# Expert phase of an attention and mixture-of-experts block: second layer with stationary weights, weights and biases fetched by transfers inside the chip

## The reference

```python
x = x + layernorm(attention(layernorm(x), w_kv_down, w_kv_up, w_q, w_out))
x = x + layernorm(ffn(layernorm(x), centroids, gamma, beta, W1, b1, W2, b2))

def ffn(x, ...):            # 8 experts, F = 512
    expert = argmax(feats @ centroids.T)            # one expert for each token
    alpha  = sigmoid(sum(feats * centroids[expert]))
    # the sublayer of expert e:
    #   h = layernorm(xs) * gamma[e] + beta[e]
    #   xs + relu(h @ W1[e].T + b1[e]) @ W2[e].T + b2[e]
    return alpha * y_expert + (1 - alpha) * feats
```

## Time and profile before

| what | value |
|---|---|
| median of 3 runs | 1291.23 us (1290.55 to 1293.27) |
| profiled execution, its own time | 1290.58 us |
| its span, first to last instruction | 1286.4 us |
| PE busy | 1221.9 us, 95% |
| DVE, ACT, POOL busy | 1130.4, 1062.5, 924.2 us |
| expert phase | from the first load of rows at 1101.8 us to the end of the span |

### The profile page before, as it was taken

The page is one execution under the profiler, slowest core; times in us unless marked ns, Lnnn a source line. Parts: engine busy times, 40 slices in busy tenths (PEclk is TensorE's granted clock), DMA queues, the critical chain, the costliest instruction groups (busy, mean ns, idle before and its releaser), DMA issues.

```text
span 1286.4 us, 42145 instructions
## 1 busy us (share of the span) xinstructions
PE 1221.9 (95%) x12784; PEld 1105.4 (86%) x12785; DVE 1130.4 (88%) x4457; ACT 1062.5 (83%) x3244; POOL 924.2 (72%) x1495
## 2 busy tenths in 40 slices
PE   7999999999999999999999999999999997599992
PEld 6888888888888888888888888888888886599982
DVE  5999999999999999999999999999999995488873
ACT  4999898999999999999999999999999893466661
POOL 4577777777777777777777777777777665067775
PEclk8999999999999999999999999999999997799997
DMA  5000000000000000000000000000000003333320
GB/s 228 6 10 18 16 16 16 16 16 16 16 16 16 16 16 16 16 16 16 16 16 16 16 16 16 13 16 14 15 16 13 15 15 123 98 97 101 96 84 13
DMA packets 39233, 43.03 MB, mean 33 GB/s; under 512 B 4802, under 2 KB 35398, under 8 KB 38800
## 3 DMA queue, kind: packets, MB, share of 16 engines
q1 hardware_dynamic: 33536, 29.43, 7.6%
q0 software_dynamic: 5648, 13.00, 2.7%
HBM read 25.16 MB, written 18.16 MB: 34 GB/s over the span
## 4 chain that ended last, share of the span: by engine, by line
PE 86%; issue 5%; POOL 3%; DVE 1%; ACT 1%; SPq 1%; DMA 1%; POOLq 0%; ACTq 0%; DVEq 0%
PE psZU L682 17%; PE psS L605 14%; PE psZU L697 14%; PE psP L649 10%; PE psZU L685 7%; PE psT L619 5%; PE psT L620 5%; PE psT L621 5%; PE psS L292 3%; POOL out L456 2%; PE psZU L306 2%; PE psT L306 1%; PE psP L584 1%; PE psM L736 1%; PE psM L727 1%
## 5 line engine op out<-in xcount | busy, mean ns | idle before, releaser
L1219 POOL TENSOR_TENSOR softmax<-softmax,rinv 128x256 f32<-128x256 f32 (+1 forms) x512 | 413.2, 828 | 213.8 <-DVE rinv L947 213.0
L781 ACT ACTIVATE softmax<-softmax,nmax 128x128 f32<-128x128 f32 (+1 forms) x1024 | 453.8, 451 | 9.1 <-DVE nmax L923 8.3
L923 DVE CUSTOM_DVE_ANT_0 softmax<-psS,mask 128x128 f32<-128x128 f32 (+1 forms) x1024 | 321.6, 352 | 5.6 <-PE psS L605 1.1
L932 DVE TENSOR_TENSOR p_both<-psP,p_both 128x768 fp32r<-128x768 f32 x256 | 243.8, 952 | 0.9 <-ACT p_both L745 0.9
L745 ACT ACTIVATE t_hi<-psT 128x512 fp32r<-128x512 f32 x256 | 153.0, 598 | 84.0 <-PE psT L621 78.0
L911 DVE TENSOR_TENSOR t_lo<-psT,t_hi 128x512 fp32r<-128x512 f32 x256 | 175.3, 685 | 41.9 <-ACT t_hi L745 40.8
L745 ACT ACTIVATE p_both<-psP 128x768 fp32r<-128x768 f32 x256 | 206.6, 807 | 2.3 <-PE psP L649 2.3
L781 ACT ACTIVATION_READ_ACCUMULATOR softmax<-softmax,nmax 128x1 f32 x1024 | 199.1, 194 | 0.0
L952 DVE TENSOR_TENSOR z_lo<-psZU,z_hi 128x512 fp32r<-128x512 f32 x256 | 175.3, 685 | 20.0 <-ACT z_hi L745 18.1
L605 PE MATMUL psS<-t_hi,t_lo 64*128 64x128 f32 (+1 forms) x1024 | 164.5, 317 | 0.4 <-DVE nmax L923 0.4
L682 PE MATMUL psZU<-p_both,xk_hi 128*128 128x512 f32 x512 | 160.7, 395 | 0.0
(11 more groups left out here) (197 smaller groups left out, 3192.0 us busy)
## 6 DMA issues: line engine op xcount, KB each, us to landing
softmax<-routed_rows SPq DMA_DIRECT2D x39, 260.0 KB, 2.7
routed_rows<-padr SPq DMA_DIRECT2D x8, 520.0 KB, 4.9
wx<-ffn_w SPq DMA_DIRECT2D x2, 2058.0 KB, 13.0
xin<-x SPq DMA_DIRECT2D x32, 128.0 KB, 2.2
xres<-x SPq DMA_DIRECT2D x32, 128.0 KB, 2.1
out<-wq_s,ids POOLq DMA_INDIRECT x78
wup_s<-wup SPq DMA_DIRECT2D x1, 1024.0 KB, 5.9
routed_rows<-pay,dst POOLq DMA_INDIRECT x64
```

Of the source, the lines that this page charges most:

```text
L781: last = nc.scalar.activation(prob[:, pb, h, a:z], nscore[:, (s - lag) % 2, h, a:z], ACT.Exp, bias=nmax[:, pb, h, q:q + 1], scale=-1.0, ac ...
L923: last = v.tensor_tensor_reduce(nscore[:, n1, h, a:z], psS[:, h, a:z], mask[:, a:z], -1.0, -MASKED, ALU.add, ALU.min, nmax[:, p1, h, q:q + 1])
L932: v.tensor_tensor(by_half(p_lo, s % 2), psPh, by_half(p_hi, s % 2).bitcast(F32), ALU.subtract).then_inc(S["p_split"], 1)
L1219: last = g.tensor_tensor(pr, pr, rinv[:, p2, :, q:q + 1].broadcast_to([P, 2, z - a]), ALU.mult)
```

## The change

PE now takes the second layer's weights as stationary operand and the hidden activations, 256 tokens wide, as the moving one, for tile s-2. The result `psY` has channels on the partitions. ACT adds the bias b2, one number for each partition, while it copies the result to `yt` (tile s-3), and PE turns `yt` back (two transposes to `psO`, tile s-3). DVE's part with gain and statistics is now for tile s-4, DVE's and ACT's normalisation and POOL's add for tile s-5, POOL's scatters for tile s-6. There is one slot more at the end (`rest + 6`).

The weights no longer come by ACT copies or by PE's addressing. SP issues two more transfers for each tile, from SBUF to SBUF: the split W1 of the expert into `w1st` (two buffers, 4096 bytes for each partition), and b1, W2 and b2 together into `w2st` (four buffers, 2068 bytes for each partition). It reads the expert from `table` once for both. The first waits until the first layer of the tile before last is done, the second until the tile four earlier has left its buffer. `b2row`, `picks` and `b1st`, and all that prepared them (L711, L745 with `b2row`, L1012 and L1014), are gone. Left out of the diff below are the renumbered lags of DVE and POOL and DVE's lines of `b2row`.

```diff
@@ -261,13 +261,26 @@
                     sp.wait_ge(S["pad_stored"], 16 * E)
                 sp.dma_start(fin[:, s], rows[bass.ds(row, T), :].rearrange("(t p) c -> p t c", p=P)
                              ).then_inc(f_loaded[s], 16)
+                if live(2):
+                    sp.wait_ge(S["h_done"], m0 + s - 1)
+                elif s == 0:
+                    sp.wait_ge(S["w1_split"], E)
+                e = sp.value_load(table[0:1, bass.ds(m0 + s, 1), 1], min_val=0, max_val=E - 1)
+                sp.dma_start(w1st[:, s % 2].rearrange("p m f -> p (m f)").bitcast(F32),
+                             w1[:, bass.ds(e, 1)].rearrange("p a m f -> p (a m f)").bitcast(F32)
+                             ).then_inc(w1_loaded[s % 2], 16)
+                if live(4):
+                    sp.wait_ge(S["yt_ready"], m0 + s - 3)
+                    sp.wait_ge(S["relu_d"], m0 + s - 3)
+                elif s == 0:
+                    sp.wait_ge(S["bias_added"], 1)
+                sp.dma_start(w2st[:, s % 4, :], wx[:, bass.ds(e, 1), B1:].rearrange("p a c -> p (a c)")
+                             ).then_inc(w2_loaded[s % 4], 16)
 
             ffn_phases(sp, slot)
 
         def ffn_pe(pe):
             mm = nc.tensor.matmul
-            pe.wait_ge(S["table_ready"], 1)
-            pe.wait_ge(S["b2_split"], 1)
 
             def slot(m0, n0, s, live):
                 if live(0):
@@ -277,12 +290,10 @@
                     for t in range(2):
                         last = nc.tensor.transpose(psN[:, t * P:(t + 1) * P], fin[:, s, t, 0:P], ident[:])
                     last.then_inc(S["n_tr"], 1)
-                if live(2):
-                    e = pe.value_load(table[0:1, bass.ds(m0 + s - 2, 1), 1], min_val=0, max_val=E - 1)
                 if live(1):
 
                     pe.wait_ge(S["nt_ready"], m0 + s)
-                    pe.wait_ge(S["w1st_ready"], m0 + s)
+                    pe.wait_ge(w1_loaded[(s - 1) % 2], 8 * m0 + 16 * ((s + 1) // 2))
                     if live(2):
                         pe.wait_ge(S["relu_a"], m0 + s - 1)
                         pe.wait_ge(S["relu_d"], m0 + s - 1)
@@ -292,21 +303,26 @@
                             last = mm(psH[:, j, :], w1st[:, b, m, j * P:(j + 1) * P], nt[:, b, :],
                                       start=(n == 0), stop=(n == 2))
                     last.then_inc(S["h_done"], 1)
-                if live(2):
-
-                    pe.wait_ge(S["relu_a"], m0 + s - 1)
-                    pe.wait_ge(S["relu_d"], m0 + s - 1)
+                if live(3):
+
+                    pe.wait_ge(S["yt_ready"], m0 + s - 2)
                     if live(4):
                         pe.wait_ge(S["g_steps"], 2 * (m0 + s - 3) - 1)
                     for t in range(2):
-                        y = psY[s % 2][:, t, 0:P]
-                        mm(y, picks[:], b2row[:, bass.ds(e, 1), :].rearrange("p a c -> p (a c)"), start=True, stop=False)
-                        for j in range(FB):
-                            a = W2 + j * P
-                            last = mm(y, hid[:, s % 2, j, t * P:(t + 1) * P],
-                                      wx[:, bass.ds(e, 1), a:a + P].rearrange("p a c -> p (a c)"),
-                                      start=False, stop=(j == FB - 1))
-                    last.then_inc(S["y_done"], 1)
+                        last = nc.tensor.transpose(psO[:, t, 0:P], yt[:, t * P:(t + 1) * P], ident[:])
+                    last.then_inc(S["y_tr"], 1)
+                if live(2):
+
+                    pe.wait_ge(S["relu_a"], m0 + s - 1)
+                    pe.wait_ge(S["relu_d"], m0 + s - 1)
+                    pe.wait_ge(w2_loaded[(s - 2) % 4], 4 * m0 + 16 * ((s + 2) // 4))
+                    if live(3):
+                        pe.wait_ge(S["yt_ready"], m0 + s - 2)
+                    for j in range(FB):
+                        a = FB + j * P
+                        last = mm(psY[:, 0, :], w2st[:, (s - 2) % 4, a:a + P], hid[:, s % 2, j, :],
+                                  start=(j == 0), stop=(j == FB - 1))
+                    last.then_inc(S["yt_done"], 1)
 
             ffn_phases(pe, slot)
 
@@ -323,33 +339,28 @@
                     if live(2):
                         act.wait_ge(S["h_done"], m0 + s - 1)
                     cp(nt_hi[:, s % 2, :], psN[:, 0:T]).then_inc(S["nt_hi_done"], 1)
-                if live(4):
-                    b, sf = s % 2, (s - 4) % FU
-                    act.wait_ge(S["gmv_ready"], m0 + s - 3)
+                if live(3):
+                    act.wait_ge(S["yt_done"], m0 + s - 2)
+                    if live(4):
+                        act.wait_ge(S["y_tr"], m0 + s - 3)
+                    nc.scalar.activation(yt[:], psY[:, 0, :], ACT.Identity,
+                                         bias=w2st[:, (s - 3) % 4, W2W - 1:W2W]).then_inc(S["yt_ready"], 1)
+                if live(5):
+                    b, sf = (s - 5) % 2, (s - 5) % FU
+                    act.wait_ge(S["gmv_ready"], m0 + s - 4)
                     for t in range(2):
                         last = nc.scalar.activation(gsd[:, b, t:t + 1], gmv[:, b, t, 1:2], ACT.Sqrt,
                                                     bias=fin[:, sf, t, C_EPS:C_EPS + 1])
                     last.then_inc(S["gsd_ready"], 1)
-                if live(0):
-                    e = act.value_load(table[0:1, bass.ds(m0 + s, 1), 1], min_val=0, max_val=E - 1)
-                    if live(2):
-                        act.wait_ge(S["h_done"], m0 + s - 1)
-                    cp(w1st[:, s % 2].rearrange("p m f -> p (m f)"),
-                       w1[:, bass.ds(e, 1)].rearrange("p a m f -> p (a m f)")).then_inc(S["w1st_ready"], 1)
                 if live(1):
                     act.wait_ge(S["h_done"], m0 + s)
-                    act.wait_ge(S["b1st_ready"], m0 + s)
+                    act.wait_ge(w2_loaded[(s - 1) % 4], 4 * m0 + 16 * ((s + 3) // 4))
                     if live(3):
-                        act.wait_ge(S["y_done"], m0 + s - 2)
+                        act.wait_ge(S["yt_done"], m0 + s - 2)
                     for j in range(2):
                         last = nc.scalar.activation(hid[:, (s - 1) % 2, j, :], psH[:, j, :], ACT.Relu,
-                                                    bias=b1st[:, (s - 1) % 4, j:j + 1])
+                                                    bias=w2st[:, (s - 1) % 4, j:j + 1])
                     last.then_inc(S["relu_a"], 1)
-                if live(0):
-                    if live(4):
-                        act.wait_ge(S["relu_d"], m0 + s - 3)
-                    cp(b1st[:, s % 4, :], wx[:, bass.ds(e, 1), B1:W2].rearrange("p a c -> p (a c)")
-                       ).then_inc(S["b1st_ready"], 1)
 
             ffn_phases(act, slot)
 
...
@@ -705,12 +716,6 @@
                     first_bias(range(s - 1, s))
                 if not live(0) and s == 7:
                     first_bias(range(E // 2, E))
-                if not live(0) and s == 4:
-                    pe.wait_ge(S["nmax_ready"], 2 * PAIRS * NB)
-                    for e in range(E):
-                        last = mm(psS[:, e // 4, (e % 4) * P:(e % 4 + 1) * P],
-                                  wx[:, e, B2:B2 + 1].broadcast_to([P, P]), ident[:], start=True, stop=True)
-                    last.then_inc(S["b2_turned"], 1)
                 if s == 1 and not live(2):
                     pe.wait_ge(S["xn_ready"], 2)
                     turn_x()
@@ -798,11 +803,6 @@
                     if live_b(2):
                         act.wait_ge(S["a_tr"], b0 + db - 1)
                     cp(at[:], psU[:, 0:T]).then_inc(S["u_copied"], 1)
-                if not live(0) and s == 5:
-                    act.wait_ge(S["b2_turned"], 1)
-                    for n in range(2):
-                        last = cp(b2row[:, 4 * n:4 * n + 4, :].rearrange("p e c -> p (e c)"), psS[:, n, :])
-                    last.then_inc(S["b2_hi_done"], 1)
                 if live(0):
                     act.wait_ge(S["t_ready"], g0 + s + 1)
                     if live(2):
...
```

More of the change, by code:

```diff
@@ L195, in block_kernel @@
             "p (b m f) -> p b m f", b=2, m=2)
[L196 to L199, removed]
+        W2W = FB + FB * P + 1
+        w2st = sb("w2st", [P, 4, W2W])
         assert 2 * HD == 2 * FB * T and HD // P == 2 * FB
         hid = wup_s[:].rearrange("p (b j t) -> p b j t", b=2, j=FB)
+        yt = sb("yt", [P, T])
         gst = sb("gst", [P, 2, 6])
@@ L206, in block_kernel @@
         grs = sb("grs", [P, 2, 2])
-        for n in """pads_ready pad_stored ends_ready table_steps table_ready w1_hi_done w1_split w1st_ready b1st_ready
-            b2_turned b2_hi_done b2_split
-            nt_hi_done nt_ready relu_a relu_d n_tr h_done y_done g_steps gmv_ready gsd_ready
+        for n in """pads_ready pad_stored ends_ready table_steps table_ready w1_hi_done w1_split
+            nt_hi_done nt_ready relu_a relu_d n_tr h_done yt_done yt_ready y_tr g_steps gmv_ready gsd_ready
```

(49 more changed lines are left out.)

24 lines of the change are left out of this document (11 added, 13 removed).

## The result

Median 1305.67 us after (1302.58 to 1307.37, 4 runs), 1292.22 before on the same chip (1290.55 to 1293.27, 4 runs): ratio 1.0114, 95% interval 1.0098 to 1.0131. By the medians the change costs 13.5 us, where I had forecast 3.3. The profiled execution took 1307.3 with a span of 1302.9, against 1290.58 and 1286.4 before.

The account below looks back on a forecast made before the run. It took a loop over POOL's scatters with late PE signals, 3.89 us a tile, as the bound, not PE's 3.6. -3.2+0.9+1.7+1.7+2.2=+3.3 on 1291.2 gave 1294.5 us, range 1281 to 1315.

Parts of the forecast that it names:

- Ahead of the phase: Before the expert phase: dropped matmuls, ACT copies and DVE steps let the pads' addresses come earlier, -3.2 us.
- PE's sum: PE's work per tile in the expert phase: 3.65 us against 3.64 before, nothing gained or lost.
- Rival B: Expert phase: PE's signal leaves POOL's scatters, so PE's pace of 3.6 us a tile applies; 1282.7 us, chance 0.24.
- The loop over SP's queue: Expert phase: next rows queue behind SP's wait for the first layer; 3.95 us a tile against 3.89, +1.7 over 29 tiles.
- H to landing: From PE's end of the first layer, which SP awaits, to the next rows' arrival, including slow register loads: 6.0 us.
- The first tiles: Start of the expert phase: tile 1's rows come later, +0.9 us; tiles 2 to 7 run at the transfers' pace, +1.7.
- The end: End of the expert phase: one more turn between load and scatter starts POOL's last run later, +2.2 us (0 to 3.9).
- What was named to look for: Expert-phase signs: transposes waiting for rows, register loads over 0.3 us, DMA share near 0.8, pads' addresses 3.2 us earlier.
- C: Expert phase: transfers queue like the pads, rows landing in 4.9 us, 4.65 a tile; 1317 us, chance 0.16.
- Rival A: Expert phase: the old loop over DVE and POOL's scatters stays the bound at 3.89 us a tile; 1292.5 us, chance 0.24.
- the loop of 7.77: Expert phase before: ACT's xt_hi, DVE, POOL's add and scatter, late PE signal, xt_hi again; 7.77 us for two tiles.
- The rule for one transfer: Skill's DMA price applied to SP's three transfers per tile: all there 4.4 us after first issue, so their loop would not bind.

Follow-up runs that it names:

- second trace of after: The changed kernel, unaltered, run again as a control on another chip: 1303.78 us, ratio 1.0159 to the kernel before.
- half the bytes: The changed kernel without copying the low part of the first layer's split weights, half of each such transfer: 1294.53 us, ratio 1.0113 to the kernel before.
- the rows ahead: The changed kernel with SP fetching each tile's rows one tile earlier, behind the slot's weight transfers: 1289.16 us, ratio 1.0066 to the kernel before.
- ACT's copy: The changed kernel with the first layer's weights copied by ACT again, only the second layer's by transfer: 1289.57 us, ratio 1.007 to the kernel before.
- one scatter: The kernel before with one of POOL's two scatters per tile, half the output rows unwritten; run twice: 1275.49 us, ratio 0.9942; 1274.48, ratio 0.9945.

## Why the prediction was right in direction and wrong in size

1305.7 lies inside the range of 1281 to 1315, but outside the forecast's own 1291.5 to 1300. The cost was four times the forecast's +3.3. The direction came out, to which I had given 0.40, and so did the path over SP's queue; the sum did not.

- **Ahead of the phase,** forecast -3.2: right. The pads' register loads began at 1076.4 in place of 1080.0 (-3.6), DVE's `best` ran at 1073.60 in place of 1075.14, and the first `xt_lo` came 3.98 earlier. One pair cannot show it so closely: in the four traces of the unaltered kernel before the first `xt_lo` stands anywhere from 1102.8 to 1106.0. But the eight traces without the change (mean 1104.7) and the six with it (1100.2) do not overlap.
- **PE's sum,** forecast 3.65: right as a sum of work, wrong as the pace. The eight passes, taken at 1.80, measured 1.74 to 1.91, and the two more transposes add 0.22 where they do not wait. The failed step is "DVE's and POOL's operations move by one tile and keep number and size: 0": by that move the output's transposes came to wait for DVE's `xin` of the same slot, and the row measured 3.85 and not 3.6. Against the 3.9 of the first pair this cost nothing; against the 3.63 that the kernel before can have it is 0.22 a tile. Rival B named no such wait; its 3.6 stands in one interval of each trace and in no stretch.
- **The loop over SP's queue,** forecast 3.95 a tile: the mechanism is as written, its size the main miss. Forecast H to landing 6.0. Measured 1168.21+2.70-1164.32=6.6 in the first trace. It failed in the instructions, not in the data. I had let the rows start behind `w1`'s and `w2`'s bytes; in fact the transfer landed in 2.70, as alone, but was issued at H+3.9, where 0.8+0.37+0.55+0.8 and 0.4 for slow register loads gave 2.9. A weights instruction is 0.50, not 0.37; the load of the rows' address 0.76 in the median, as under the pads; and moves and checks stand between. After the landing the rest is 2.0 to 2.2, not 1.85, as the transposes take 0.43 behind rows that have only just landed. In the second trace of after the transfer was issued at H+3.4 and landed at H+6.2. There it starts 2.68 after `w1`'s instruction (1174.75-1172.07), in the first 3.23 (1168.21-1164.98): there two periods are 8.5, 4.25 a tile. The term was +1.7 for 29 tiles; the 30 intervals measured +13.2.
- **The first tiles,** forecast +0.9 and +1.7: +5.5. The first two intervals took 1.4 more than before, the third 2.5, the eighth, where the hardware loop begins, 1.05. The failed step is "will run at the transfers' pace: 5x0.35": the term leaves out how long the first turn of the loop is. The third `xt_lo` stands at 1109.28 and the fourth at 1115.95, 6.67 apart. In between the first layer of tile 0 ended at 1107.90 (the first H that SP waits for), the rows of tile 3 were issued at H+3.2, and landed 3.92 later. PE was meanwhile at the lower clock level (1.2 GHz; granted 0.50 until 1113.6; it had stood idle 9.9 and 3.2 us for the rows of the first two tiles), and its eight passes took 2.84, so that of the landing only 0.5 shows as a wait.

```profile
1111.09 3.92 DMA softmax<-routed_rows
```
```profile
1111.72 2.84 PE L323 MATMUL psT<-wup_s,w2st 128*128 128x256 f32 x8
...
1115.05 0.45 PE L291 MATMUL psZU<-ident,softmax 128*128 128x128 f32 x2 [0.50 <-DMA softmax<-routed_rows]
```

  Either nearly suffices alone. With half the bytes the clock stood at full level from 1104.9 on, and PE stood idle for the rows instead; the interval was 6.0 (the granted clock is third from the end in the first line):

```profile
1105.00:1112.00 7.00, 4.72 (x32) 4.09 (x31) 2.04 (x6) 2.22 (x6) 0.00 (x0) 1.00 0.61 197
```
```profile
1110.76 0.44 PE L291 MATMUL psZU<-ident,softmax 128*128 128x128 f32 x2 [1.77 <-DMA softmax<-routed_rows]
```

  With the rows ahead no transpose waited there, but the clock stood at 0.50 until 1108.8, and it was 5.7. With ACT's copy, without both, it was 4.0. The lower level also comes without the change: in the kernel before this interval was 4.2, but 6.37 in one trace with one scatter, where the clock rose only at 1115.1.
- **The end,** forecast +2.2: +1.7, right in size and not in its path. POOL's last unbroken run did not begin one short turn later: it began 3.4 us behind the last `xt_lo` and no longer 8.3, with six tiles in it in place of four, some 3.3 us each.
- **What was named to look for:** transposes waiting for the DMA of the rows, register loads over 0.3 (0.76), a share near 0.8 (0.75 to 0.80) and earlier pads were all there. "Over 4.3, it is C" was met in the number and not in the mechanism: C had the landing at 4.9, and it stayed at 2.7 in the middle of the phase.
- **Rival A** had no ground left: in after, `xt_hi` starts 0.31 behind the second transpose, and the loop of the earlier trace rows does not close.
- **What bounded the kernel before:** the loop of 7.77 was in the trace and was read rightly, but its late signal is a condition of the run and no fixed cost. I had one trace and took it for the kernel. In the session without it the ratio was 1.0159 against 1.0114; the two intervals just overlap (1.0124 to 1.0193 and 1.0098 to 1.0131).
- **The rule for one transfer:** the Trainium skill ("DMA: Bandwidth & Descriptors", "Anatomy of one DMA", about 2.0 us plus bytes at 436 GB/s) states it for transfers that GpSimd issues; these are SP's, which I had not said. As an estimate it gives 2.6 for the rows, and the chain's 2.70 agrees. It gave H+5.2 in the forecast because I had put the three transfers on it and left out what SP needs before the third, H+3.9 and H+3.4 here; the rule has no term for that.

## What to carry to other kernels

A transfer whose buffer comes free late must not stand in front of one that could go early: put it behind, or fetch the other one a step further ahead (here 0.30 of the 0.62 us a tile that the change cost). Price a queue of transfers by its instructions as well, register loads under traffic and all, and not only by bytes and landing. When stages move by a tile, look at which waits now fall into the same slot, and at buffers that went from two to one: here that made PE's 3.6 us of work a row of 3.85.

## What the runs showed of the hardware that I had not expected

- PE's semaphore signals are late in some runs and never in others, whatever the kernel. In the kernel before `xt_hi` followed the transposes by 1.13 us or by 0.42 with a scatter in progress in both, 3.9 or 3.63 us a tile. I did not find what it hangs on.
- A register load from SBUF on SP took 0.26 us in the kernel before (share 0.32). The load of the rows' address, right behind the weights' transfers, took 0.27, 0.52 and 0.76 to 0.85 us in the median at shares of 0.51, 0.67 and 0.75 to 0.85, while the second one, right after a wait, stayed at 0.26 to 0.29. Share and place in the queue were not varied apart.
- Copies within SBUF and loads of rows together ran at 288 GB/s and a share of 0.85, with a landing for the rows of 2.9 us in the median against 2.7 alone.
